# The states' term of a delta-rule layer's output product on 32x32 tiles of TensorE instead of 64x64 tiles

## The reference

```
x = x + 0.5 * ffn(layernorm(x))
x = x + attn(layernorm(x))
x = x + 0.5 * ffn(layernorm(x))
```

```
S  = S * exp(g_t)
dv = (v_t - k_t . S) * b_t
S  = S + k_t (outer) dv
o_t = q_t . S
```

## Time and profile before

| what | value |
|---|---|
| runs, us | 1762.78, 1771.76, 1785.77 (median 1771.76) |
| profiled execution, first to last instruction | 1760.8 us |
| PE busy | 1679.1 us, 95%, 49152 matmul records |
| PE's weight loads busy | 1411.3 us, 80%, 49152 records |
| VectorE, ScalarE, GpSimd busy | 72%, 68%, 26% |
| mean granted TensorE clock | 0.968 of 2.4 GHz |
| instruction queue q8 | 388 packets, 6.36 MB |

### The profile page before, as it was taken

The page is one execution under the profiler, slowest core; times in us unless marked ns, Lnnn a source line. Parts: engine busy times, 40 slices in busy tenths (PEclk is TensorE's granted clock), DMA queues, the critical chain, the costliest instruction groups (busy, mean ns, idle before and its releaser), DMA issues.

```text
span 1760.8 us, 108854 instructions
## 1 busy us (share of the span) xinstructions
PE 1679.1 (95%) x49152; PEld 1411.3 (80%) x49152; DVE 1263.6 (72%) x3718; ACT 1203.0 (68%) x2241; POOL 461.1 (26%) x389
## 2 busy tenths in 40 slices
PE   5699999999999999999999999999999999999886
PEld 4487888888888888888888888888888888887775
DVE  4866777887767788777778777777877777887441
ACT  7666776677677667777766777676676767667445
POOL 0223332223333222333322233322223332222301
PEclk9889999999999999999999999999999999999876
DMA  3000000000000000000000000000000000000000
GB/s 121 1 4 4 5 16 16 16 16 16 10 10 16 16 16 16 16 4 16 16 16 16 16 16 4 16 17 16 16 16 16 4 16 10 10 10 10 10 10 13
DMA packets 21614, 26.95 MB, mean 15 GB/s; under 512 B 2208, under 2 KB 20768, under 8 KB 21152
## 3 DMA queue, kind: packets, MB, share of 16 engines
q1 hardware_dynamic: 21152, 19.99, 3.5%
HBM read 11.60 MB, written 8.39 MB: 11 GB/s over the span
## 4 chain that ended last, share of the span: by engine, by line
PE 88%; issue 6%; DVE 4%; ACT 2%; POOL 1%; ACTq 0%; DVEq 0%; POOLq 0%
PE ps L242 40%; PE ps L224 15%; PE ps L233 10%; PE ps L217 7%; PE ps L443 3%; PE ps L210 3%; PE ps L394 2%; PE ps L347 2%; PE ps L532 2%; PE ps L538 2%; PE ps L362 1%; DVE CV L1071 1%; ACT L621 0%; ACT L618 0%; DVE TZ L1093 0%
## 5 line engine op out<-in xcount | busy, mean ns | idle before, releaser
L1071 DVE SCALAR_TENSOR_TENSOR CV<-ps,cw,CV 128x256 f32<-128x256 f32 x576 | 233.9, 475 | 49.4 <-ACT CV L664 48.9
L242 PEld LDWEIGHTS ps<-MQ,S 64*64 64x64 f32 x4096 | 145.3, 139 | 60.3 <-issue 45.9
L1178 DVE TENSOR_TENSOR MQ<-GQ,ps 128x384 f32<-128x384 f32 x32 | 17.7, 554 | 227.9 <-PE ps L242 227.9
L242 PE MATMUL ps<-MQ,S 64*64 64x16 f32 x4096 | 170.6, 212 | 1.8 <-ACT S L615 1.8
L986 POOL TENSOR_TENSOR ST<-GB,msk 128x512 f32<-128x512 f32 x32 | 41.6, 1300 | 469.1 <-ACT GB L883 469.1
L951 POOL TENSOR_TENSOR XK<-XK 128x512 f32<-128x512 f32 x32 | 33.3, 1040 | 470.2 <-ACT XK L705 470.2
L615 ACT ACTIVATE S<-SA,pair 128x512 f32<-128x512 f32 x128 | 81.9, 710 | 96.5 <-DVE SA L1103 96.5
L242 PEld LDWEIGHTS ps<-VT,WP 32*32 32x32 f32 x8192 | 89.5, 108 | 70.1 <-issue 58.0
L618 ACT ACT_TABLE_LOAD x112 | 143.7, 1283 | 2.5 <-DVE prod L1411 0.6
L621 ACT ACT_TABLE_LOAD x111 | 142.4, 1283 | 1.9
L217 PE MATMUL ps<-XK,w_k_ffn 128*128 128x256 f32 x512 | 136.6, 413 | 4.9 <-DVE XK L1058 4.8
(11 more groups left out here) (138 smaller groups left out, 3878.7 us busy)
## 6 DMA issues: line engine op xcount, KB each, us to landing
X<-in_x SPq DMA_DIRECT2D x32, 256.0 KB, 2.8
out_x<-X SPq DMA_DIRECT2D x32, 256.0 KB, 2.3
KQI<-in_blocks SPq DMA_DIRECT2D x2, 256.0 KB, 4.2
w_r_ffn<-in_wT_r_ffn SPq DMA_DIRECT2D x1, 256.0 KB, 3.3
w_k_ffn<-in_wT_k_ffn SPq DMA_DIRECT2D x1, 256.0 KB, 3.5
w_v_ffn<-in_wT_v_ffn SPq DMA_DIRECT2D x1, 256.0 KB, 5.3
w_k<-in_wT_k SPq DMA_DIRECT2D x1, 256.0 KB, 4.4
w_q<-in_wT_q SPq DMA_DIRECT2D x1, 256.0 KB, 4.7
```

The source lines that it names most:

```text
L242: last = mm(ps[rows, o:o + n], stat[rows, pk].rearrange("p s c -> p (s c)"), mov[rows], **flags)
L1071: stt(d4[:, m], src, cw[:, i, m, tap:tap + 1], d4[:, m], ALU.mult, ALU.add).then_inc(signal, 1)
```

## The change

The states' term gets two slots instead of four. `S4` (four slots) becomes `S2` (two slots), the waits on `s_slots` count two per group instead of four, and `in_slots` therefore issues two ACTIVATEs per group instead of four, with the two-slot mask. `pairs` sees two slots and issues four matmuls of 32x32 per pack for this term instead of two of 64x64. No segment moves in any engine's order.

```
-        K4, KD4, S4 = (sb(n, [P, PACKS, HT, C]) for n in ("K4", "KD4", "S4"))
+        K4, KD4 = (sb(n, [P, PACKS, HT, C]) for n in ("K4", "KD4"))
+        S2 = sb("S2", [P, PACKS, 2, C])
...
             def o_product(g, h):
                 if h == 0:
-                    pe.wait_ge(s["s_slots"], 4 * g + 4)
+                    pe.wait_ge(s["s_slots"], 2 * g + 2)
...
                 for pk in part:
-                    pairs(PS["o"] * BANK + pk * C, C, S4, pk, MQ[g % 2][:, pk, U:], start=(pk == 0), stop=False,
+                    pairs(PS["o"] * BANK + pk * C, C, S2, pk, MQ[g % 2][:, pk, U:], start=(pk == 0), stop=False,
                           skip_group_check=True)
...
-                in_slots(S4, SA[g % 2][:], s["s_slots"])
+                in_slots(S2, SA[g % 2][:], s["s_slots"])
...
             def chain(g, n):
                 ve.wait_ge(s["ch_ps"], NCH * g + n + 1)
                 if n == 0 and g >= 2:
-                    ve.wait_ge(s["s_slots"], 4 * g - 4)
+                    ve.wait_ge(s["s_slots"], 2 * g - 2)
                 if n == NCH - 1 and g:
-                    ve.wait_ge(s["s_slots"], 4 * g)
+                    ve.wait_ge(s["s_slots"], 2 * g)
```

## The result

The changed kernel takes 1854.22 us (median of four runs, 1850.72 to 1867.5) against 1767.27 us for the kernel before, measured beside it (1760.79 to 1785.77). The ratio is 1.053 with a 95% interval of 1.047 to 1.059: 87 us slower. The forecast was 1824 us, 3% slower, within 1765 to 1880 us.

The account below looks back on a forecast made before the run. PE's work bounds the kernel, with instruction delivery a near second bound that would bind the dense stretch (o_product 0 to end of d_products): 30 x 1.72 = 52 us more, ends and ScalarE 0, so 1771.8 + 52 = 1824 us, range 1765 to 1880.

Parts of the forecast that it names:

- The price of the tiles: On PE, two o_products take 1.20 us instead of 1.88, saving 2.7 us of work per group.
- One block per group: In PE's instruction queue, one block of 256 instructions more per step, about 420 packets instead of 388.
- The cadence: When PE has used up delivered instructions, it gets one block (128 matmuls with their loads) per 4.02 us.
- The store: 0.71 block already delivered when the dense stretch (o_product 0 to end of d_products) begins; stretch then 26.8 us against 25.09.
- The clock: Rival, chance 0.05: PE's clock also falls, in one step of ten, adding about 60 us: 1885 us.
- The base: The sum starts from the runs' median of 1771.8 us, 11 us over the profiled execution of 1760.8 us.
- ScalarE and the ends: Two ACTIVATEs fewer per group, worth 0 to 2 us, taken as 0; in the drain PE's saving is eaten: 0.
- The rival in which delivery never binds: Whole saving on PE arrives, 30 x 2.7 = 81 us off plus up to 4 at the ends: 1687 us; chance 0.13.

Follow-up runs that it names:

- the ballasted kernel: Changed kernel with ffn1_v, ffn3_k, ffn3_r, k_squares and o_squares each computed twice: 1961.92 us, against 1972.68 us for the kernel before with the same additions.
- The added work: Changed kernel with three 128x512 matmuls done again per step (k_squares three times, o_squares twice): 1875.20 us.

## Why the prediction was right, and what it sized wrongly

The direction and its cause hold. In the prediction's order:

- *The price of the tiles*: 1.20 us for two o_products; 1.22 us measured in the ballasted kernel. Right. The 25 ns per matmul that the prediction cites from the Trainium skill ("TensorE: Matmul & The Clock Gate", section "Wait — 56ns, not 53.3ns?") have no part here either: 64 small matmuls of a pair's states' term and 64 of its values' term ran in 1.22 us, under 10 ns each.
- *One block per group*: 420 packets, 388 + 32, and 53248 records. Right.
- *The cadence*: 4.02 us was taken from three intervals. In the six dense stretches at full clock a packet arrived per 3.74 us. The term was 7% too long.
- *The store*: 0.71 block was taken from one place of the drain. Counted from the packets, the six full-clock stretches begin with 0.67 block in the mean, the other 20 with 0.80, so this term was about right, though it varies from 0.1 to 1.4 from one stretch to the next. What the sum had wrong is the end: it let a stretch use the store up, and 0.39 block is left. (7.38 - 0.67 + 0.39) x 3.74 = 26.6 us. The short cadence and the store left over cancel, which is luck: the dense stretch at full clock was forecast as 26.8 us and is 26.8 us.
- *The clock*: this is the term that was mis-sized. I put it into a rival of 5%, as something that would happen in one step of ten, and left it out of the sum. It happens in 20 of 26 dense stretches, and these are 1.5 us longer than the others at like pauses. Over all steps that is 1.5 x 20 / 26 = 1.2 us a step, about 35 us in 30 steps. The full-clock stretches are 26.8 - 24.9 = 1.9 us longer than before, 57 us in 30 steps, where the sum had 52. Together they make the profile's 92 us. The added work, which raised the clock to 0.960, agrees with idle time bringing it down; no run separates idle time from the rest.
- *The base*: the sum stood on a median of 1771.8 us, 11 us over the profiled span. With the fourth run the median is 1767.3 us, and each run's own span is 2 us under its time. These 4.5 us made the forecast look nearer than it was: the change costs 87 us, and 52 were summed.
- *ScalarE and the ends*: taken as nothing. ACT's busy time fell by 39 us, and the steady steps account for the profile's 92 us without it. No run tests either term by itself.
- *The rival in which delivery never binds* is excluded by the pauses. What the Trainium skill says in "Runtime: NRT & Kernel Launch", section "Instruction fetch mechanics", that fetching is hidden, the trace refutes for this stream: 107 us of pauses. Its block of 256 instructions agrees with 420 packets for 106496 records, 254 each.

## What to carry to other kernels

Count PE's instructions per microsecond, not only its busy time: a stretch of small tiles that needs more than about 256 instructions (128 matmuls with their loads) per 3.8 us will pause, and then tiles that are cheaper for the array make the kernel slower. Look for "issue" pauses at equal distances in the timeline of the kernel before; a few short ones mean that the edge is near. Where it is, prefer changes that save work and no instructions (fewer changes of tile form, larger tiles in one of two terms), and keep long matmuls spread between the bursts.

## What the runs showed of the hardware that was not expected

- PE's instructions arrive in packets of 256 that never start less than 3.2 us apart in the two kernels, and a starved PE resumes 1.2 to 1.6 us behind a packet's end.
- The store is so small that a burst of 88 small matmuls behind a b_product and chain can empty it: moving one projection of 1.9 us by two segments cost 70 us, most of it through the clock.
- The clock can fall although PE is busy for most of the time and no such pause is longer than 2.7 us: it stood at 0.51 right behind 5 us in which PE had been busy for 3.6. Stretches with the same number of records and like pauses kept 1.00, so what decides between them stays open.
- Redundant matmuls raised the mean clock from 0.932 to 0.960 and cost a quarter of their own length, which is estimated as 84 us: about 24 us went into idle time, and about 40 us came back by the clock.
